# Rotary attention: the half-turned q and k by copies 64 partitions away and GpSimd instead of permuted projections, and another order of SyncE's queue

## The reference

```python
x = x + attn_a(norm(x))   # causal softmax; heads 0 to 2 weigh a third of the keys by 1.6
x = x + ffn(norm(x))      # ternary weights: silu(a) * b, two gelu layers 512 x 512, 512 -> 128
x = x + attn_b(norm(x))   # no mask, rotary q and k
x = x + ffn(norm(x))
# rotary of attn_b, on pairs of neighbouring features of a head
rx = xx * cos - xy * sin
ry = xx * sin + xy * cos
```

## Time and profile before

| | |
|---|---|
| median of 3 runs | 2131.85 us (2125.42 to 2132.75) |
| the profiled execution | 2132.76 us, its span 2131.0 us |
| TensorE busy | 1936.5 us, 91% |
| VectorE busy | 1719.3 us, 81% |
| ScalarE busy | 1480.6 us, 69% |
| GpSimd busy | 1097.7 us, 52% |
| mean granted TensorE clock | 0.967 of full speed |
| DMA | 136.7 MB moved, 64 GB/s in the mean |

### The profile page before, as it was taken

How to read it: one execution, slowest core, us unless ns; L and a number is a source line. 1 busy time by engine, 2 the same in 40 slices (tenths; PEclk the granted TensorE clock), 3 DMA queues, 4 the chain that set the end, 5 groups by cost and what they waited for, 6 DMA issues and landing times.

```text
span 2131.0 us, 43057 instructions
## 1 busy us (share of the span) xinstructions
PE 1936.5 (91%) x16196; PEld 979.3 (46%) x16196; DVE 1719.3 (81%) x2342; ACT 1480.6 (69%) x2641; POOL 1097.7 (52%) x1553
## 2 busy tenths in 40 slices
PE   3889998898889999997899999999999978999998
PEld 1333433343347777763222222222222226777776
DVE  4888887887748888876898989899898926888883
ACT  1477777776866666652688888888887875666665
POOL 5777777776545556565233333334333014555554
PEclk9899999999989999998899999999999989999999
DMA  7456665655210000012434433444444100000000
GB/s 177 96 118 127 119 128 117 125 119 112 40 47 1 1 1 1 1 32 58 86 78 86 92 73 72 85 90 87 92 79 97 23 13 12 16 11 15 11 16 16
DMA packets 106357, 136.71 MB, mean 64 GB/s; under 512 B 21153, under 2 KB 90018, under 8 KB 100002
## 3 DMA queue, kind: packets, MB, share of 16 engines
q1 hardware_dynamic: 106146, 133.89, 31.1%
HBM read 67.78 MB, written 55.58 MB: 58 GB/s over the span
## 4 chain that ended last, share of the span: by engine, by line
PE 47%; POOL 11%; SPq 11%; DMA 10%; issue 8%; DVE 8%; ACT 4%; POOLq 0%; ACTq 0%; DVEq 0%
PE ps_score L1451 20%; PE ps_out L1059 7%; PE ps_max L1451 5%; PE ps_score L1001 4%; DMA o_num<-o_raw 4%; SPq L580 4%; DVE negmax L872 3%; PE ps_max L1019 3%; DMA d_stack<-parts 3%; PE ps_out L1451 3%; ACT prob L987 2%; POOL xhat L322 2%; SPq L558 2%; PE ps_max L1100 2%; DMA stack_q<-nm_rows 2%
## 5 line engine op out<-in xcount | busy, mean ns | idle before, releaser
L987 ACT ACTIVATE prob<-ps_score 128x512 f32<-128x512 f32 x1664 | 898.9, 597 | 197.0 <-PE ps_score L1001 179.3
L872 DVE TENSOR_REDUCE negmax<-ps_max 128x2 f32<-128x1024 f32 (+1 forms) x896 | 908.0, 1065 | 136.9 <-PE ps_max L1036 73.1
L1059 PE MATMUL ps_out<-prob,v_aug 128*9 128x256 f32 (+2 forms) x6656 | 515.9, 390 | 28.2 <-ACT o_raw L950 26.0
L1451 PE MATMUL ps_score<-h,w_hi 128*128 128x512 f32 x2048 | 501.5, 398 | 10.0 <-POOL h L1223 8.2
L1451 PEld LDWEIGHTS ps_score<-h,w_hi 128*128 128x128 f32 x2048 | 381.6, 188 | 104.9 <-POOL h L1223 10.8
L1001 PE MATMUL ps_score<-stack_q,stack_k 50*128 50x512 bf16 (+3 forms) x2048 | 359.1, 351 | 56.9 <-ACT prob L987 34.4
L1019 PE MATMUL ps_max<-stack_k,stack_q 48*128 48x512 bf16 (+3 forms) x2048 | 344.7, 355 | 51.0 <-DVE negmax L872 32.4
L708 POOL TENSOR_SCALAR_AFFINE_SELECT prob<-prob 128x256 f32<-128x256 f32 (+1 forms) x448 | 188.3, 440 | 141.7 <-ACT prob L987 141.3
L1211 POOL TENSOR_TENSOR h<-h3f,h 128x512 fp32r<-128x512 f32 x128 | 192.2, 1510 | 130.9 <-ACT h L1363 130.9
L1001 PEld LDWEIGHTS ps_score<-stack_q,stack_k 50*128 50x128 bf16 x2048 | 105.3, 94 | 312.7 <-ACT prob L987 236.0
L1059 PEld LDWEIGHTS ps_out<-prob,v_aug 128*9 128x9 f32 x6656 | 106.0, 89 | 305.0 <-ACT prob L987 146.2
(11 more groups left out here) (114 smaller groups left out, 2106.9 us busy)
## 6 DMA issues: line engine op xcount, KB each, us to landing
d_stack<-parts SPq DMA_DIRECT2D x128, 192.0 KB, 2.8
stack_q<-d_stack SPq DMA_DIRECT2D x64, 384.0 KB, 5.6
stack_k<-d_stack SPq DMA_DIRECT2D x64, 384.0 KB, 6.1
d_stack<-parts SPq DMA_DIRECT2D x128, 128.0 KB, 2.8
d_stack<-parts SPq DMA_DIRECT2D x128, 64.0 KB, 2.4
o_num<-o_raw SPq DMA_DIRECT2D x128, 64.0 KB
o_rden<-d_rden SPq DMA_DIRECT2D x128, 64.0 KB
x<-in_x SPq DMA_DIRECT2D x16, 256.0 KB, 6.9
```

What stands on the lines that cost most here:

```text
L872: last = dve.tensor_reduce(m["negmax"][:, t, :, p], banks[:, :, at:at + w], AX.X, ALU.max, negate=True)
L987: act.activation(prob(b, i)[:, o], act_bank("score", 2 * i + o), ACT.Exp).then_inc(s["prob"], 1)
L1059: last = pe.matmul(m["ps_out"][32 * g:32 * g + HD + 1, out:out + w], m["v_aug"][b % VALUES][:, j, 4 * G + g, :], prob(b, beat)[:, g % 2, l ...
L1451: mm = pe.matmul(to, w[:, cols], moving(part), start=begin and i == 0, stop=last and i == len(pairs) - 1)
```

## The change

The second copies of wq and wk go, and with them qr, kr and `turn`. The rows of q and k are put in another order: the even features of all heads are rows 0 to 63, the odd ones rows 64 to 127, so that the partner of a row is 64 partitions away. `project` now writes q + bias alone. A new `swap` on SyncE copies the two halves of `qf` crosswise into `turned` with two DMAs. A new `rotate`, on GpSimd (for k of batch 0 on VectorE), multiplies `turned` by sin and `qf` by cos and adds them. The stores take all 128 partitions at once, three DMAs instead of six. SyncE's queue gets another order, for both attention stages. In the table, GpSimd's middle and low of k come before `norm`, q's first part at 27.

```diff
-ROTARY_AT = {"k": 3, "nm1": 3, "kr": 6, "v": 15, "proj": 14, "xT": 19, "nm0": 23, "q": 23, "qr": 27,
+ROTARY_AT = {"k": 3, "nm1": 3, "v": 15, "proj": 14, "xT": 19, "nm0": 23, "q": 23,
...
-             "P_q1": 24, "P_q2": 31, "P_k1": 11, "P_k2": 15, "P_nm0": 19, "P_o": 0, "D_stats": 16, "D_clear": 18,
-             "D_q": 24, "D_qr": 28, "D_k": 4, "D_kr": 7, "A_v": 16, "D_bias": 2, "D_inv": 15, "D_proj": 15, "A_nm1": 4,
+             "P_q1": 27, "P_q2": 31, "P_k1": 9, "P_k2": 13, "P_nm0": 19, "P_o": 0, "D_stats": 16, "D_clear": 18,
+             "D_q": 24, "D_k": 4, "A_v": 16, "D_bias": 2, "D_inv": 15, "D_proj": 15, "A_nm1": 4,
...
+    def swap(sp, b, name, i):
+        sp.wait_ge(s[f"{name}_main"], b + 1)
+        for at in range(0, P, SWAP):
+            sp.dma_start(m["turned"][at:at + SWAP, i], m["qf"][at ^ SWAP:(at ^ SWAP) + SWAP, i])\
+                .then_inc(s[f"{name}_swap"], 16)
...
     def store(sp, b, name, i):
         sp.wait_ge(s["parts"], count(2, b, i + 1))
-        for o in range(2):
-            parts = m["parts"][64 * o:64 * (o + 1), i]
-            rows = m["d_stack"][b % 2, i, o].rearrange("t d p n -> (d p) t n")
-            for part, (lo, hi) in enumerate(((0, 3), (3, 5), (5, 6))):
+        parts = m["parts"][:, i]
+        rows = m["d_stack"][b % 2, i].rearrange("t d o p n -> (d o p) t n")
+        for part, (lo, hi) in enumerate(((0, 3), (3, 5), (5, 6))):
...
     def sync(sp, n):
+        if on(n, 3):
+            numerators(sp, n - 3)
+        if rotary and on(n, 0) and not early("k", n):
+            swap(sp, n, "k", 1)
+        if on(n, 2):
+            aug(sp, 1, n - 2)
         if on(n, 0):
             load(sp, n, "stack_q", "stored_q", 0)
         if causal and on(n, -X_AHEAD):
             load_x(sp, m, a, n + X_AHEAD)
-        if on(n, 2):
-            aug(sp, 1, n - 2)
-        if on(n, 3):
-            numerators(sp, n - 3)
         if n > 0 and on(n, 0):
             store(sp, n, "stored_k", 1)
         if on(n, 3):
             store_reciprocals(sp, n - 3)
         if on(n, 0):
             load(sp, n, "stack_k", "stored_k", 1)
+        if on(n, 1):
+            aug(sp, 0, n - 1)
+        if rotary and on(n, -1):
+            swap(sp, n + 1, "q", 0)
         if on(n, 3):
             spread_reciprocals(sp, n - 3)
-        if on(n, 1):
-            aug(sp, 0, n - 1)
         if on(n, -1):
             store(sp, n + 1, "stored_q", 0)
...
+    def rotate(eng, b, name, i):
+        eng.wait_ge(s[f"{name}_swap"], count(16 * (P // SWAP), b, 16 * (P // SWAP)))
+        eng.tensor_tensor(m["turned"][:, i], m["turned"][:, i], m["rope"][:, 2 * i + 1], ALU.mult)
+        eng.tensor_tensor(m["qf"][:, i], m["qf"][:, i], m["rope"][:, 2 * i], ALU.mult).then_inc(s[f"{name}_turn"], 1)
+        eng.wait_ge(s[f"{name}_turn"], b + 1)
+        eng.tensor_tensor(m["qf"][:, i], m["qf"][:, i], m["turned"][:, i], ALU.add).then_inc(s[name], 1)
...
-        dve.scalar_tensor_tensor(out=m["qf"][:, i], in0=bank, scalar=m["bias_col"][:, i:i + 1],
-                                 in1=m["rope"][:, 2 * i], op0=ALU.add, op1=ALU.mult).then_inc(s[f"{name}_main"], 1)
-
-    def turn(dve, b, name, i):
+        dve.tensor_scalar(m["qf"][:, i], bank, m["bias_col"][:, i:i + 1], None, ALU.add).then_inc(s[f"{name}_main"], 1)
```

Where the rotary stage starts, inside the feed-forward stage, the same products go. k of batch 0 is projected one place earlier, k of batch 1 right after q of batch 1, `sync_fill` issues the swaps of batches 0 and 1 (q and k each), and GpSimd splits k of batch 1 before `norm` of batch 2 instead of after it:

```diff
     def pool_fill(pool):
...
         ones(pool, range(1, VALUES))
+        high(pool, 1, "k", 1)
+        middle_low(pool, 1, 1)
         norm(pool, 2)
         negated_max_parts(pool, 0, 0)
-        high(pool, 1, "k", 1)
-        middle_low(pool, 1, 1)
```

More of the change, by code:

```diff
@@ L419, in attention @@
     else:
-        names += ("q_main", "qr_ps", "q_turn", "k_main", "kr_ps", "k_turn")
+        names += ("q_main", "q_swap", "q_turn", "k_main", "k_swap", "k_turn")
     s = {n: sem(f"{tag}_{n}") for n in names}
-    W_Q, W_K, W_V, W_QR, W_KR, W_O = range(6)
-    EARLY = {"q": 2, "qr": 2, "k": 2, "kr": 2, "v": 1} if rotary else {}
+    W_Q, W_K, W_V, W_O = range(4)
+    EARLY = {"q": 2, "k": 2, "v": 1} if rotary else {}
     LOOP_END = B + 2
@@ L810, in parts_on_vector @@
         rest = m["turned"][:, i]
-        dve.wait_ge(s[f"{name}_turn"], b + 1)
-        dve.tensor_tensor(m["qf"][:, i], m["qf"][:, i], m["turned"][:, i], ALU.add).then_inc(s[name], 1)
+        rotate(dve, b, name, i)
         dve.wait_ge(s[name], b + 1)
@@ L841, in project @@
             return
-        dve.scalar_tensor_tensor(out=m["qf"][:, i], in0=bank, scalar=m["bias_col"][:, i:i + 1],
-                                 in1=m["rope"][:, 2 * i], op0=ALU.add, op1=ALU.mult).then_inc(s[f"{name}_main"], 1)
-    def turn(dve, b, name, i):
-        dve.wait_ge(s[f"{name}r_ps"], b + 1)
-        wait(dve, s[name], b)
-        dve.scalar_tensor_tensor(out=m["turned"][:, i], in0=linear_bank(name + "r", b),
-                                 scalar=m["bias_col"][:, 2 + i:3 + i], in1=m["rope"][:, 2 * i + 1],
-                                 op0=ALU.add, op1=ALU.mult).then_inc(s[f"{name}_turn"], 1)
+        dve.tensor_scalar(m["qf"][:, i], bank, m["bias_col"][:, i:i + 1], None, ALU.add).then_inc(s[f"{name}_main"], 1)
     def whole_bias(dve, bank):
@@ L899, in vector @@
                     project(dve, n + 1, "q", 0)
-                if rotary and i == AT["D_qr"]:
-                    turn(dve, n + 1, "q", 0)
             if on(n, 0):
@@ L904, in vector @@
                     project(dve, n, "k", 1)
-                if rotary and i == AT["D_kr"] and not early("kr", n):
-                    turn(dve, n, "k", 1)
                 if (n, i) == (0, AT["D_bias"]):
@@ L1146, in misc_work @@
                 linear(pe, n, n + 1, "q", W_Q)
-            if rotary and i == SLOT["qr"]:
-                linear(pe, n, n + 1, "qr", W_QR)
         if not on(n, 0):
@@ L1154, in misc_work @@
             linear(pe, n, n, "k", W_K)
-        if rotary and i == SLOT["kr"] and not early("kr", n):
-            linear(pe, n, n, "kr", W_KR)
         if i == SLOT["v"]:
@@ L1175, in attention @@
                widen_bias=widen_bias, norm=norm, high=high, middle_low=middle_low, weighted=weighted,
-               statistics=statistics, parts_on_vector=parts_on_vector, project=project, turn=turn, whole_bias=whole_bias, invert=invert,
+               statistics=statistics, parts_on_vector=parts_on_vector, project=project, whole_bias=whole_bias, invert=invert,
                residual=residual, flag_of_weights=flag_of_weights, copy_xT=copy_xT, values=values, turn_x=turn_x, fill_linear=fill_linear,
@@ L1324, in vector_layer @@
             if fill:
-                fill["turn"](dve, 0, "k", 1)
                 fill["parts_on_vector"](dve, 0, "k", 1)
@@ L1343, in vector_layer @@
         after.vector(dve, 1, 5, 7)
-        fill["turn"](dve, 1, "q", 0)
+        fill["project"](dve, 1, "k", 1)
         after.vector(dve, 1, 7, 9)
         add_y(dve, first + B - 1)
-        after.vector(dve, 1, 9, 14)
-        fill["project"](dve, 1, "k", 1)
-        after.vector(dve, 1, 14, 16)
-        fill["turn"](dve, 1, "k", 1)
-        after.vector(dve, 1, 16)
+        after.vector(dve, 1, 9)
     def gelu(act, b, k, f, reader):
@@ L1583, in rows_of_heads @@
 def rows_of_heads():
-    return np.array([(2 * p + o) * HD + d for o in range(2) for d in range(HD) for p in range(PAIRS)])
+    return np.array([(2 * p + o) * HD + 2 * c + e for e in range(2) for c in range(HD // 2) for o in range(2) for p in range(PAIRS)])
 def rows_of_output():
```

65 lines of the change are left out of this document (27 added, 38 removed).

## The result

| | median | runs | ratio, 95% interval |
|---|---|---|---|
| before | 2130.57 us | 2125.42 to 2132.75 (4) | |
| after | 2063.38 us | 2061.71 to 2065.22 (4) | 0.9688, 0.9668 to 0.9709 |

The changed kernel is 3.1% faster. The prediction was 2063.0 us. The total came out, but several of the terms under it did not, by 5, 4 and 3 us in both directions; that it came within 0.4 us is luck. The rest of this text is about the terms.

A forecast was written before the change was run, and what follows sets the result against it. TensorE was taken to pace the rotary step, and ScalarE's wait for the numerators to stand out in the causal stage; 2132.8 - 33 (rotary) - 32 (causal) - 5 (rotary start) = 2063 us, range 2040 to 2100.

The forecast's parts named there:

- (a): Rotary step: two f32 projections (qr, kr) go, -2.12 us of TensorE; VectorE's changed `project` costs nothing.
- (b): Rotary step: half 0's maxima rows go ahead of the four spreading DMAs, removing a TensorE wait, -0.48 us.
- (c): Rotary step: numerators go ahead of a load and half 1's maxima rows, -0.6 us of TensorE's wait on ps_out's copy.
- (d): Rotary step: GpSimd's rotation with two copies in front makes nm_parts late for TensorE, a stall of 0.8 us.
- y: Rotary stage: time from issue of the second swap copy to its landing, taken as 2.8 us from the stores.
- (e): Stores of 128 rows: 1.9 us less of SyncE's queue, shortening nothing that is last in the steady loops.
- (f): Causal stage: sums start earlier, ScalarE's wait for numerators goes, -32 us (between -20 and -44), step of 31.1 possible.
- (g): Start of the rotary stage, 965 to 1030 us: fewer projections against added multiplications, -5 us, between -10 and 0.
- The slow one: Rival: swap copies share rings and engines with loads and stores and land late, stalling both chains; up to 2195 us; chance 0.06.
- GpSimd late: Rival: rotary swap copies land in 4.24 us like the numerators, rotary gain shrinks to 14 us, 2082 us; chance 0.20.
- late `aug`: Rival: causal stage, half 1's maxima rows behind the sums cause a new wait, gain 12 instead of 32, 2083; chance 0.12.
- "better" case: Rival: short landings (2.3 us) and full causal knock-on, gains of 41 and 44 us, 2043 us; chance 0.12.

The follow-up runs named there:

- k after norm: Changed kernel with k's second parts operation placed behind the next norm on VectorE and GpSimd (place 15 instead of 13); 2125.16 us.
- sums late: Changed kernel with the sums' five DMAs behind k's copies, the maxima's rows of half 1 and the loads; 2131.51 us.
- q's copies late: Changed kernel with q's two copies issued after the four spreading DMAs instead of ahead of them; 2100.57 us.

## Why the prediction was right, and where it was not

The sum was 33 + 32 + 5 us of gain; measured are 38 (32.5 in twelve steps, 5.5 behind them), 27.9 and 1.6. All three are within their own bounds.

- **(a) Two products fewer.** Mis-sized in what came through. The products are worth 2.1 us of TensorE as priced, and the step lost 1.6 (45.1 to 43.5 with order and stores in both). Left out was that TensorE would then wait 0.5 us a step more for the other engines. VectorE's new `project` takes 0.750 us as the old one did, so costing the difference at nothing was right.
- **(b), (c) Maxima's rows and numerators first, together 1.1 us a step.** The size was right: order alone, in the kernel before, gave 1.1, and the two waits named are the ones that went: 0.65 us a step on the copy, 0.5 on the maxima's rows. The cause given for (b), their place ahead of the spreading, fell. SyncE reaching that part of its queue earlier, which the stores bring about as well, fits all three runs; the wait's cause was not isolated further.
- **(d) A stall of 0.8 us on GpSimd's chain.** There is none. The chain itself holds: 14.5 us from q's projection to the end of nm_parts, against 12.3 + y = 14.7 by the prediction with the measured y. y was 2.35 instead of 2.8, taken from the stores; the small `den` would have been the better row. And TensorE comes later than I let it, 15.3 us after the projection instead of 14.4, having waited 0.56 us for ScalarE's exponentials and 0.37 for a copy on the way. Here the errors of (a) and (d) cancel: -2.12 + 0.8 = -1.3 was forecast for the rotation, -1.6 came.
- **(e) The stores at nothing.** The step that failed. "In the steady loops this shortens nothing that is last" was not so in the kernel before, where they alone gave 43.5 us: the store of q stands ahead of the load, the load ahead of the maxima's rows and the sums, and those were the last to arrive. On top of the new order it was nearly so: the rotary step stays at 45.1, the last copy moves by 2 us, the medians by 7 (2091.49 to 2084.86), and in the changed kernel by 0 to 10. I counted 1.9 us of queue and looked for a reader of the stores, not for what is queued behind them. The total survived only because (c) and (f) had already claimed the same microseconds for the order.
- **(f) The causal wait, -32 us.** -27.9. The step is 31.24 us in the steady part instead of 31.1. The wait goes as described and `aug` 1 keeps its room. The part had no term for TensorE's clock, which rose from 0.96 to 0.99 in the mean of 100 to 560 us. By an estimate from these two, 460 us x 0.03 = 14 us of work at full clock, so part of the 27.9 may be clock and not the wait itself; no run tells them apart.
- **(g) The start, -5 us.** -1.6, at the weak side of its bounds. The changed kernel's VectorE timeline shows one of the costs named, with GpSimd busy beside it throughout:

```profile
920.04 1.65 DVE L680 TENSOR_TENSOR turned<-turned,rope 128x512 f32<-128x512 f32 x1
921.61 1.09 DVE L681 TENSOR_TENSOR qf<-qf,rope 128x512 f32<-128x512 f32 x1
922.74 1.53 DVE L683 TENSOR_TENSOR qf<-qf,turned 128x512 f32<-128x512 f32 x1
...
925.73 1.65 DVE L837 TENSOR_TENSOR turned<-qf,parts 128x512 f32<-128x512 f32 x1
```

The three of the rotation take 4.3 us against 3 x 0.69 by the short case of the earlier trace rows, and the last one shown took 0.69 us in the kernel before (VectorE at 951.4), with GpSimd idle from 951.1 to 953.5. The Trainium skill ("SBUF — State Buffer", who interferes with whom) says that such an operation and one of GpSimd's that reads SBUF exclude each other; this trace agrees, up to 1.65 us for 0.69. No run isolated it.

**The rivals.** The slow one, the copies landing late, did not happen, but "k after norm" shows it in the same kernel with one table entry changed: a landing of 5.3 us. "GpSimd late" did not happen for q, whose copies landed in 2.35 us; k's came near its y, 3.2 to 3.9, and had room for it. The late `aug` is real too, two groups further down the queue. The "better" case had the landing right (2.3 for q's copies) and not the 41 and 44 us that it built on it.

## What to carry to other kernels

A DMA that nobody is waiting for still costs its issue time to everything behind it on the same in-order queue; price a shorter store by what is next in the queue, not by its reader. Two edits that relieve the same queue need not add: here they gave 36 and 44 us alone and 49 together, and the order became worth 35 us again when the copies joined the queue. And when a transfer's place in the queue is chosen, look at what was issued just ahead of it: a copy of 128 KB landed in 2.35 us behind two rows of maxima (8 KB each), in 3.2 to 3.9 behind four eight-row copies and in 4.5 to 5.9 soon after a load of 2 x 384 KB.

## What was not expected of the hardware

- **A stall of TensorE can cost more than its length.** Behind all twelve waits of 3.2 to 4.1 us in the rotary stage of "sums late" the granted clock was between 0.50 and 0.72 in the mean of the next 6 us, and a beat took 1.94 us for 1.1. Shorter waits went either way: four of eight of 1.8 to 1.9 us in "q's copies late" were followed by it, one of 2.61 us in "k after norm" was not, and in the kernel before one of 1.65 us was (0.50 for 3 us behind 1227.87). So a delay did not cost its size alone: 2.1 us of mean wait cost 3.2 a step, 3.0 cost 5.0.
- **Copies between partitions.** Two DMAs of 64 partitions, 2 KB to each partition, landed in 2.2 us at best, 2.4 in the median of 64 and 4.0 at most. The Trainium skill ("DMA: Bandwidth & Descriptors", the anatomy of one DMA) gives about 2.0 us fixed plus bytes over 436 GB/s for DMAs that GpSimd issues, by which an estimate for 128 KB is 2.3 us. SyncE issues these, and the trace agrees with the figure for q's copies. k's copies are the slower ones, and six of eight of them lost the difference when they were issued ahead of the numerators.
